# One batched graph kernel: the transposed operator scaled by a row instead of transposed on TensorE

## The chip, the core and the metric

The kernel runs on one core of one Trainium2 chip. The metric is the device time of one execution in microseconds (us). The time before is 292.79 us, the median of three runs (292.77 to 293.01). The engines in the profile are PE (TensorE matmuls), PEld (TensorE's weight loads), DVE (VectorE), ACT (ScalarE), POOL (GpSimd) and SP (SyncE, which here only issues DMAs).

## The reference

There are 64 graphs of 128 nodes, with 256 features each. For each graph, H is the 128 x 128 matrix of "adj is not zero", w is the first row of adj, and

```python
Dn = where(H @ w > 0, 1 / (H @ w), 0)            # one number per node
Be = 1 / H.sum(axis=0)                           # one number per hyperedge
def conv(x, W, b): return Dn * (H @ (Be * (H.T @ (x @ W.T)))) + b
h = layer_norm(relu(conv(x, W1, b1)))            # 256 -> 512 features
y = conv(h, W2, b2)                              # 512 -> 256 features
out = layernorm(x + (y + x))
```

With S = H B H^T (B the diagonal of Be) and D the diagonal of Dn, both convolutions apply A = D S to the nodes. S is symmetric, so A^T = S D: row i of A is row i of S times D_i, and column i of A^T is column i of S times D_i.

## The kernel before

The 64 graphs are handled in 16 groups of 4 (`PER = 4`, `G = 16`). Each engine has its own instruction stream, written out by hand, with semaphores between the streams; nothing is scheduled by a compiler, so the order in the code is the order on the engine. The main loop runs over i = 0 to 15; here one pass of it is called **stage i**. Stage i finishes group i and prepares the groups after it.

For a group j the steps are: `make_h` (DVE: H in bf16), `turn_h` (from group 3 on a DMA transpose issued by SP), `read_ht` (ACT: H^T, with the column sums), `make_b` (DVE: 1/column sums, `binv`), `make_htb` (ACT: B H^T), `copy_w` (POOL: w as a last column), `make_s` (PE: S and the node degrees, in PSUM tile `bank_s`), `make_d` (DVE: `dinv`, the D of the group, one value per node on its partition), `make_a` (ACT: A = D S, four instructions, one per graph), `turn_a` (PE: four transposes of A, against `ident`), `read_at` (ACT: A^T from PSUM into `at_sb`). A^T is what TensorE needs as weights: `make_u` multiplies it with x, and `make_y` with the hidden layer. The scaling D must be on the row index of A, which in S's own layout is a number per partition (cheap: `scale=dinv`), and in A^T's layout a number per column.

After that come `make_u` (PE), `split_u` (ACT and DVE: u as a high and a low part), `make_v` (PE, four blocks k = 0 to 3, three products each), `relu` and `square` (ACT), `split_r` (POOL makes `r_hi`, DVE `r_lo`), `add_pair` and `add_pairs` (DVE: sums of squares, `q_sb`), `turn_q` (PE transposes `q_sb`), `sum_q` (ACT), `make_g` (PE, one per graph), `make_var1` (DVE, four tiny instructions per half of a group), `inverse_std1` (POOL: a power of -0.5), `read_g` (DVE), `make_y` (PE, in two halves), `make_z` (DVE: y + 2 * `xb_sb`), `take_stats2` and `make_var2` (DVE), `inverse_std2` (POOL: a power and `shift2`), `normalise` (ACT), `store` (SP). `add_b2` (POOL) makes `xb_sb` = x + b2/2.

TensorE's order in a middle stage i is: make_g of graphs 0 and 1, make_v(i+1, 0), make_g of graph 2, make_v(i+1, 1), make_g of graph 3, make_v(i+1, 2), make_v(i+1, 3), **turn_a(i+2)**, make_y(i, 0), make_y(i, 1), make_s(i+3), make_u(i+2), turn_q(i+1). Two of its waits: the two halves of make_y use the PSUM banks that the last two blocks of make_v used, so half 1 waits until `relu` has read block 3:

```python
pe.wait_ge(g_ready, i * 2 + (half + 1))
pe.wait_ge(relu_ready, (i + 1) * KH + 3 + half)
```

And turn_q(i+1) waits for `q_ready`, DVE's last addition of squares.

SP works through one list of DMAs in order; in stage i these are load_adj(i+6), turn_h(i+4), load_x(i+3) and store(i-1), each with its own wait, and what is behind a waiting one waits too.

## Time and profile before

| | |
|---|---|
| median of three runs | 292.79 us |
| the profiled execution | 292.85 us |
| its span, first to last instruction | 291.0 us |
| PE busy | 279.9 us (96%) |
| DVE busy | 225.9 us (78%) |
| ACT busy | 210.4 us (72%) |
| POOL busy | 137.8 us (47%) |
| granted TensorE clock, mean | 0.993 of full |
| DMA, mean | 83 GB/s |

A timeline row has its start, its duration, the engine, the line, the operation and the tiles, how many instructions it merges, and in brackets, where there was one, the idle time before it with what ended it. Start times are from the span's start. Durations of neighbours overlap a little, since an instruction starts before the one ahead of it has drained; so the time that an instruction takes from its engine is read as the distance from its start to the next start, and its duration says when its result is there.

### The profile page before, as it was taken

The numbers are of one execution on the slowest core, as the hardware profiler recorded it, in microseconds if no ns is written. First come the engines' busy times: TensorE is split into PE (matmuls) and PEld (weight loads), VectorE is DVE, ScalarE is ACT, GpSimd is POOL, SyncE is SP. The second block draws the span as 40 slices with busy tenths as digits, with TensorE's granted clock in tenths as the row PEclk, the third lists the DMA queues.
The fourth block names the chain that finished last, engine by engine and source line by source line (L and its number), as shares of the span: only waits on it lengthen the run. The fifth ranks groups of instructions, "written<-read, shape, count | busy, mean of one in ns | idle before, by whom it ended". The sixth has DMA issues, their size and how long they took to land.

```text
span 291.0 us, 5897 instructions
## 1 busy us (share of the span) xinstructions
PE 279.9 (96%) x1866; PEld 254.4 (87%) x1866; DVE 225.9 (78%) x647; ACT 210.4 (72%) x621; POOL 137.8 (47%) x178
## 2 busy tenths in 40 slices
PE   7799999999999999999999999999999999999991
PEld 6689979898998989898998989899898989889880
DVE  1776689696978878697878969797897969587784
ACT  3397968868696887868687886868688785764514
POOL 2223763745454563645365374535446364426332
PEclk9999999999999999999999999999999999999997
DMA  6922040523406060321506051221406101020204
GB/s 222 303 78 50 8 126 0 123 79 77 124 18 182 0 199 2 119 83 29 170 3 199 2 156 43 77 88 23 145 0 185 53 31 44 0 74 0 72 3 144
DMA packets 33511, 24.28 MB, mean 83 GB/s; under 512 B 7932, under 2 KB 33224, under 8 KB 33480
## 3 DMA queue, kind: packets, MB, share of 16 engines
q1 hardware_dynamic: 33376, 23.86, 27.7%
q8 instruction: 15, 0.25, 0.4%
q14 instruction: 16, 0.13, 0.2%
q10 hardware_dynamic: 104, 0.04, 0.1%
HBM read 13.80 MB, written 8.39 MB: 76 GB/s over the span
## 4 chain that ended last, share of the span: by engine, by line
PE 85%; DVE 7%; issue 2%; POOL 2%; ACT 2%; DVEq 0%; POOLq 0%; ACTq 0%
PE bank_v L274 28%; PE bank_v L259 10%; PE bank_g L291 9%; PE bank_g L284 9%; PE bank_g L286 9%; PE bank_v L308 8%; PE bank_s L238 5%; PE bank_s L245 2%; PE bank_g L301 2%; DVE g_sb L636 1%; POOL rstd L840 1%; PE bank_s L341 1%; DVE binv L601 1%; ACT ht_sb L429 1%; DVE r_lo L645 1%
## 5 line engine op out<-in xcount | busy, mean ns | idle before, releaser
L851 POOL TENSOR_TENSOR xb_sb<-x_sb,b_half 128x1024 f32<-128x1024 f32 x16 | 38.4, 2400 | 58.9 <-DVE r_lo L645 53.8
L284 PE MATMUL bank_g<-w_hi,r_hi 128*128 128x258 f32 x256 | 65.6, 289 | 0.0
L286 PE MATMUL bank_g<-w_lo,r_hi 128*128 128x256 f32 x256 | 63.8, 282 | 0.0
L859 POOL TENSOR_SCALAR r_hi<-r_sb 128x512 fp32r<-128x512 f32 x64 | 48.0, 751 | 27.9 <-ACT r_sb L466 27.5
L636 DVE SCALAR_TENSOR_TENSOR g_sb<-bank_g,rstd,c 128x256 f32<-128x256 f32 x64 | 28.1, 480 | 30.7 <-POOL rstd L840 30.7
L274 PE MATMUL bank_v<-u_hi,w_hi 128*128 128x512 f32 x128 | 50.8, 397 | 0.4 <-DVE u_lo L609 0.4
L274 PE MATMUL bank_v<-u_hi,w_lo 128*128 128x512 f32 x128 | 50.8, 397 | 0.0
L274 PE MATMUL bank_v<-u_lo,w_hi 128*128 128x512 f32 x128 | 50.6, 395 | 0.0
L284 PEld LDWEIGHTS bank_g<-w_hi,r_hi 128*128 128x128 f32 x256 | 48.4, 189 | 1.4
L286 PEld LDWEIGHTS bank_g<-w_lo,r_hi 128*128 128x128 f32 x256 | 48.1, 188 | 1.2
L466 ACT ACTIVATE r_sb<-bank_v,vec 128x512 f32<-128x512 f32 x64 | 43.8, 684 | 7.2 <-PE bank_v L274 6.8
L460 ACT ACTIVATE u_hi<-bank_v 128x512 fp32r<-128x512 f32 x32 | 19.2, 599 | 38.5 <-PE bank_v L259 38.5
L645 DVE TENSOR_TENSOR r_lo<-r_sb,r_hi 128x512 fp32r<-128x512 f32 x64 | 43.3, 697 | 1.0 <-POOL r_hi L859 1.0
L478 ACT ACTIVATE z_sb<-z_sb,shift,rstd 128x256 f32<-128x256 f32 x60 | 32.5, 590 | 15.3 <-POOL shift L874 15.3
L291 PE MATMUL bank_g<-w_hi,r_lo 128*128 128x258 f32 x256 | 41.3, 283 | 0.0
L473 ACT ACTIVATE sq_sb<-r_sb 128x512 f32<-128x512 f32 x64 | 40.2, 634 | 1.5
L291 PEld LDWEIGHTS bank_g<-w_hi,r_lo 128*128 128x128 f32 x256 | 35.2, 189 | 0.0
L866 POOL TENSOR_TENSOR rstd<-var,half_power 128x4 f32<-128x4 f32 (+1 forms) x17 | 17.1, 1005 | 32.1 <-DVE var L693 32.1
L259 PE MATMUL bank_v<-at_sb,x_sb 128*128 128x128 f32 x256 | 31.5, 276 | 0.8 <-ACT at_sb L454 0.7
L259 PEld LDWEIGHTS bank_v<-at_sb,x_sb 128*128 128x128 f32 x256 | 29.8, 192 | 1.6 <-ACT at_sb L454 0.9
L840 POOL TENSOR_TENSOR rstd<-stat,half_power 128x2 f32<-128x2 f32 x32 | 22.6, 706 | 17.9 <-DVE stat L626 17.9
L308 PE MATMUL bank_v<-g_sb,at_sb 128*128 128x256 f32 x120 | 28.9, 381 | 0.6 <-DVE g_sb L636 0.6
(98 smaller groups left out, 489.2 us busy)
## 6 DMA issues: line engine op xcount, KB each, us to landing
x_sb<-in_x_dram SPq DMA_DIRECT2D x16, 512.0 KB, 3.9
out_dram<-z_sb SPq DMA_DIRECT2D x15, 512.0 KB, 3.2
adj_sb<-in_adj_dram SPq DMA_DIRECT2D x16, 256.0 KB, 3.9
w_raw<-in_L_gnn_W_dram SPq DMA_DIRECT2D x2, 512.0 KB, 5.7
out_dram<-z_sb SPq DMA_DIRECT2D x2, 256.0 KB, 2.6
turned_h<-h_sb SPq DMA_TRANSPOSE x13, 2.4
b_half<-in_L_gnn_b_dram SPq DMA_DIRECT2D x1, 128.0 KB, 8.8
edge_rows<-in_adj_dram ACTq DMA_DIRECT2D x1, 32.0 KB, 3.4
```

The lines of the kernel that those rows point to most:

```text
L259: mm = pe.matmul(bank_v[:, c, graph(n)], x_sb[:, j % 3, n, graph(c)], at_sb[:, j % 3, n], start=True, stop=True)
L274: mm = pe.matmul(bank_v[:, k % 2], w[:, c, graph(k)], u[:, c], start=(m == 0), stop=(m == len(terms) - 1))
L284: pe.matmul(bank_g[:, n, 0:W2COLS], r_hi[:, i % 2, k, graph(n)], w2_hi[:, k], start=(k == 0), stop=False)
L286: pe.matmul(bank_g[:, n, 0:DOUT], r_hi[:, i % 2, k, graph(n)], w2_lo[:, k], start=False, stop=False, skip_group_check=True)
L291: mm = pe.matmul(bank_g[:, n, 0:W2COLS], r_lo[:, i % 2, k, graph(n)], w2_hi[:, k], start=False, stop=(k == KH - 1))
L308: mm = pe.matmul(bank_v[:, half, (n % 2) * DOUT:(n % 2 + 1) * DOUT], at_sb[:, i % 3, n], g_sb[:, n], start=True, stop=True)
L466: nc.scalar.activation(r_sb[:, k], bank_v[:, k % 2], ACT.Relu, bias=vec[:, k:k + 1]).then_inc(relu_ready, 1)
L473: nc.scalar.activation(sq_sb[:, k], r_sb[:, k], ACT.Square).then_inc(sq_ready, 1)
L478: ins = nc.scalar.activation(z_sb[:, i % 2, n], z_sb[:, i % 2, n], ACT.Identity, bias=shift2[:, n:n + 1], scale=rstd2[:, 0, n:n + 1])
L645: nc.vector.tensor_tensor(r_lo[:, i % 2, k], r_sb[:, k], r_hi[:, i % 2, k].bitcast(F32), ALU.subtract).then_inc(r_lo_ready, 1)
L851: nc.gpsimd.tensor_tensor(xb_sb[:, i % 2], x_sb[:, i % 3], b2_half[:, :].unsqueeze(1).to_broadcast([P, PER, DOUT]), ALU.add).then_inc(xb_r ...
L859: nc.gpsimd.tensor_scalar(r_hi[:, i % 2, k], r_sb[:, k], 1.0, 1.0, ALU.mult, ALU.mult).then_inc(r_hi_ready, 1)
```

## The change

For groups 3 to 15 (`ON_PE = 3` says how many keep the old way) A is no longer made or transposed. A^T is made directly as S D: DVE multiplies S, read from PSUM, with a tile `d_row` that holds D along the free axis, the same on every partition, and writes `at_sb`. To get D from "one value per partition" to "a row on all partitions", SP stores `dinv` (128 x 4 values) to a DRAM tensor and loads it back broadcast to 128 partitions. Around this:

- `make_a` (ACT), `turn_a` (PE) and `read_at` (ACT) go for j >= 3. The new `make_at` stands on DVE between `make_var1(i, 1)` and `read_g(i, 1)`.
- `make_d(i+2)` moves ahead of `split_u(i+1)` on DVE. `make_var1(i, 0)` moves ahead of `make_var2(i-1)`, `read_g(i, 0)` ahead of `make_h(i+4)`, and on POOL `inverse_std1(i, 0)` ahead of `inverse_std2(i-1)`.
- `add_b2` is made in two halves and one stage later: in stage i now for group i, the first half after DVE's last `split_r`, the second after `make_b(i+3)`. The last group's is made in one piece after stage 14.
- ACT's `normalise(i-1, ...)` moves back: the first half from behind block 0 to behind block 1, the second from behind block 1 to behind block 3.
- `load_x` waits for the two halves of `xb_ready`.

The diff, cut:

```diff
-        dinv = sb("dinv", [P, PER])
+        dinv = sb("dinv", [P, 2, PER])
+        d_row = sb("d_row", [P, 2, P * PER])
...
+            def store_d(j):
+                sp.wait_ge(d_ready, j + 1)
+                sp.dma_start(d_rows[j], dinv[:, j % 2]).then_inc(d_stored, 16)
+
+            def load_d(j):
+                sp.wait_ge(d_stored, 16 * (j - ON_PE + 1))
+                if j >= ON_PE + 2:
+                    sp.wait_ge(at_ready, j - 1)
+                sp.dma_start(d_row[:, j % 2], d_rows[j].rearrange("c n -> (c n)").unsqueeze(0).to_broadcast(
+                    [P, P * PER])).then_inc(d_row_in[j % 2], 16)
...
                     load_adj(i + 6)
+                if i and i + 2 < G:
+                    store_d(i + 2)
+                    load_d(i + 2)
                 if i + 4 < G:
                     turn_h(i + 4)
...
                 make_v(i + 1, 3)
-                if i + 2 < G:
-                    turn_a(i + 2)
+                if i == 0:
+                    turn_a(2)
                 make_y(i, 0)
...
-                    if i + 2 < G:
-                        make_a(i + 2)
                     if i + 3 < G:
                         make_htb(i + 3)
                     relu(i + 1, 0)
                     square(i + 1, 0)
-                    normalise(i - 1, 0)
                 relu(i + 1, 1)
                 square(i + 1, 1)
                 if i:
-                    normalise(i - 1, 1)
+                    normalise(i - 1, 0)
                 relu(i + 1, 2)
                 square(i + 1, 2)
                 relu(i + 1, 3)
-                if i + 2 < G:
-                    read_at(i + 2)
+                if i == 0:
+                    read_at(2)
                 square(i + 1, 3)
+                if i:
+                    normalise(i - 1, 1)
...
+            def make_at(j):
+
+                dve.wait_ge(d_row_in[j % 2], 16 * (j // 2 if j % 2 else (j - 2) // 2))
+                dve.wait_ge(s_made, j + 1)
+                dve.wait_ge(y_made, (j - 2) * 2)
+                nc.vector.tensor_tensor(at_sb[:, j % 3].rearrange("p (b n) c -> p b n c", b=2),
+                                        s_parts[:, :, :, 0:P],
+                                        d_row[:, j % 2].rearrange("p (c b n) -> p b n c", b=2, n=2),
+                                        ALU.mult).then_inc(at_ready, 1)
...
+            def add_b2(i, half=None):
+
+                part, n = graphs(half), len(each(half))
+                if half != 1:
+                    pool.wait_ge(x_in[i % 3], landed(i, 3))
+                    if i >= 2:
+                        pool.wait_ge(z_ready, (i - 1) * 2)
+                    if i in (0, LAST):
+                        pool.wait_ge(q_ready, i + 1)
+                    else:
+                        pool.wait_ge(r_lo_ready, (i + 1) * KH)
+                elif i + 3 < G:
+                    pool.wait_ge(b_ready, i + 4)
...
-            add_b2(0)
...
-                add_b2(i + 1)
+                for half in range(2):
+                    add_b2(i, half)
+                inverse_std1(i, 0)
                 if i:
                     inverse_std2(i - 1)
-                inverse_std1(i, 0)
...
+            add_b2(LAST)
             for half in range(2):
                 inverse_std1(LAST, half)
```

How the instructions stand on the engines, from one middle stage to the next. First DVE at the start of a stage, before: the last two `split_r` of the old stage (`r_lo`), then `split_u`, `make_d` (three rows, `degree` and `dinv`), `make_b` (two rows, `binv`), `take_stats2` and `make_var2` (`mv_sb`, `mean`, `var`), and `make_var1` from `stat` on.

```order
L645 TENSOR_TENSOR r_lo<-r_sb,r_hi 128x512 x2
L609 TENSOR_TENSOR u_lo<-bank_v,u_hi 128x512 x2
L590 TENSOR_SCALAR degree<-bank_s 128x4
L592 RECIPROCAL degree<-degree 128x4
L596 SCALAR_TENSOR_TENSOR dinv<-bank_s,degree 128x4
L601 TENSOR_SCALAR binv<-members 128x4
L604 RECIPROCAL binv<-binv 128x4
L679 BN_STATS bn_sb<-z_sb 128x6 x4
L689 BN_AGGR mv_sb<-bn_sb 128x2 x4
L692 TENSOR_SCALAR mean<-mv_sb 128x4
L693 TENSOR_SCALAR var<-mv_sb 128x4
L615 TENSOR_SCALAR stat<-bank_g 128x2
```

The same place after:

```order
L661 TENSOR_TENSOR r_lo<-r_sb,r_hi 128x512 x2
L604 TENSOR_SCALAR degree<-bank_s 128x4
L606 RECIPROCAL degree<-degree 128x4
L612 SCALAR_TENSOR_TENSOR dinv<-bank_s,degree 128x4
L625 TENSOR_TENSOR u_lo<-bank_v,u_hi 128x512 x2
L617 TENSOR_SCALAR binv<-members 128x4
L620 RECIPROCAL binv<-binv 128x4
L695 BN_STATS bn_sb<-z_sb 128x6 x4
L631 TENSOR_SCALAR stat<-bank_g 128x2
```

`make_d` now stands ahead of `split_u`, and `make_var1` directly behind the four BN_STATS.

Second, DVE in the later part of a stage, before: the end of `make_var1(i, 1)` (three of its rows), `read_g(i, 1)` (`g_sb`), then `split_r`, the first `add_pair` and the two `make_z`.

```order
L618 TENSOR_TENSOR stat<-stat 128x2
L622 SCALAR_TENSOR_TENSOR stat<-sum_sq,stat 128x2
L626 TENSOR_SCALAR stat<-stat 128x2
L636 SCALAR_TENSOR_TENSOR g_sb<-bank_g,rstd,c 128x256 x2
L645 TENSOR_TENSOR r_lo<-r_sb,r_hi 128x512
L650 TENSOR_TENSOR pair_sb<-sq_sb 128x512
L671 SCALAR_TENSOR_TENSOR z_sb<-xb_sb,bank_v 128x512 x2
```

After:

```order
L634 TENSOR_TENSOR stat<-stat 128x2
L638 SCALAR_TENSOR_TENSOR stat<-sum_sq,stat 128x2
L642 TENSOR_SCALAR stat<-stat 128x2
L756 TENSOR_TENSOR at_sb<-bank_s,d_row 128x512
L652 SCALAR_TENSOR_TENSOR g_sb<-bank_g,rstd,c 128x256 x2
L661 TENSOR_TENSOR r_lo<-r_sb,r_hi 128x512
L666 TENSOR_TENSOR pair_sb<-sq_sb 128x512
L687 SCALAR_TENSOR_TENSOR z_sb<-xb_sb,bank_v 128x512 x2
```

One instruction is added, between the last row of `make_var1` and `read_g`.

Third, POOL over the turn of a stage, before: `copy_w` (`htb_sb`), `add_b2` (`xb_sb`), `inverse_std2` (`rstd2`, `shift2`), `inverse_std1` (`rstd1`), `split_r` (`r_hi`).

```order
L834 COPY htb_sb<-edge_cols 128x4
L851 TENSOR_TENSOR xb_sb<-x_sb,b2_half 128x1024
L866 TENSOR_TENSOR rstd2<-var2,half_power 128x4
L874 TENSOR_TENSOR shift2<-mean2,rstd2 128x4
L840 TENSOR_TENSOR rstd1<-stat1,half_power 128x2
L859 TENSOR_SCALAR r_hi<-r_sb 128x512 x2
```

After:

```order
L864 COPY htb_sb<-edge_cols 128x4
L886 TENSOR_TENSOR xb_sb<-x_sb,b2_half 128x512 x2
L870 TENSOR_TENSOR rstd1<-stat1,half_power 128x2
L901 TENSOR_TENSOR rstd2<-var2,half_power 128x4
L909 TENSOR_TENSOR shift2<-mean2,rstd2 128x4
L894 TENSOR_SCALAR r_hi<-r_sb 128x512 x2
```

The piece of 128x1024 is two of 128x512, and the power of the first half of `rstd1` goes ahead of `rstd2` and `shift2`.

## Rows read from the trace of the kernel before

**Rows 1.** The page, section 1: busy us, share of the span, instructions.
```profile
PE 279.9 (96%) x1866; PEld 254.4 (87%) x1866; DVE 225.9 (78%) x647; ACT 210.4 (72%) x621; POOL 137.8 (47%) x178
```
**Rows 2.** Stretches (us): busy PE, PEld, DVE, ACT, POOL; clock, DMA share, GB/s.
```profile
128.33:144.95 16.62, 16.62 (x116) 15.29 (x114) 13.77 (x40) 13.02 (x40) 8.43 (x10) 1.00 0.31 88
60.00:240.00 180.00, 180.00 (x1215) 165.55 (x1215) 145.91 (x425) 141.88 (x427) 91.21 (x108) 1.00 0.28 82
```
**Rows 3.** Timeline of PE, end of stage 6: turn_a, make_y, then turn_q.
```profile
139.75 0.60 PE L245 MATMUL bank_s<-ident,a_sb 128*128 128x128 f32 x4
140.19 1.89 PE L308 MATMUL bank_v<-g_sb,at_sb 128*128 128x256 f32 x8
...
144.59 0.60 PE L301 MATMUL bank_g<-ident,q_sb 128*128 128x128 f32 x4
```
**Rows 4.** Timeline of PEld: the weight load of turn_q in stage 6.
```profile
144.50 0.45 PEld L301 LDWEIGHTS bank_g<-ident,q_sb 128*128 128x128 f32 x4
```
**Rows 5.** Timeline of DVE, stage 6 and the start of stage 7.
```profile
138.37 0.17 DVE L626 TENSOR_SCALAR stat<-stat 128x2 f32<-128x2 f32 x1
139.44 0.88 DVE L636 SCALAR_TENSOR_TENSOR g_sb<-bank_g,rstd,c 128x256 f32<-128x256 f32 x2 [0.89 <-POOL rstd L840]
...
140.82 1.10 DVE L650 TENSOR_TENSOR pair_sb<-sq_sb 128x512 f32<-128x512 f32 x1
...
143.76 0.69 DVE L657 TENSOR_TENSOR q_sb<-pair_sb 128x512 f32<-128x512 f32 x1
...
147.61 0.65 DVE L601 TENSOR_SCALAR binv<-members 128x4 f32<-128x4 f32 x1 [0.28 <-ACT ht_sb L429]
```
**Rows 6.** Timeline of POOL, same stretch: r_hi of block 3, then xb.
```profile
140.72 0.67 POOL L859 TENSOR_SCALAR r_hi<-r_sb 128x512 fp32r<-128x512 f32 x1 [0.73 <-ACT r_sb L466]
...
145.83 2.40 POOL L851 TENSOR_TENSOR xb_sb<-x_sb,b_half 128x1024 f32<-128x1024 f32 x1 [3.86 <-DVE r_lo L645]
```
**Rows 7.** Stage 14, which has no turn_a: timelines of PE, PEld, ACT, DVE, POOL.
```profile
272.48 2.13 PE L308 MATMUL bank_v<-g_sb,at_sb 128*128 128x256 f32 x8
...
273.48 0.73 PEld L308 LDWEIGHTS bank_v<-g_sb,at_sb 128*128 128x128 f32 x4 [0.38 <-issue]
...
272.68 0.69 ACT L466 ACTIVATE r_sb<-bank_v,vec 128x512 f32<-128x512 f32 x1
...
273.14 0.68 DVE L650 TENSOR_TENSOR pair_sb<-sq_sb 128x512 f32<-128x512 f32 x1
...
273.45 0.85 POOL L859 TENSOR_SCALAR r_hi<-r_sb 128x512 fp32r<-128x512 f32 x1 [0.76 <-ACT r_sb L466]
```
**Rows 8.** Groups by form: DVE's product-like instruction of the nearest shape.
```profile
L609 DVE TENSOR_TENSOR u_lo<-bank_v,u_hi 128x512 fp32r<-128x512 f32 x32 | 20.6, 684 | 0.4 <-ACT u_hi L460 0.4
```
**Rows 9.** DMAs: issue to landing, median us.
```profile
adj_sb<-in_adj_dram SPq DMA_DIRECT2D x16, 256.0 KB, 3.9
...
out_dram<-z_sb SPq DMA_DIRECT2D x2, 256.0 KB, 2.6
...
b_half<-in_L_gnn_b_dram SPq DMA_DIRECT2D x1, 128.0 KB, 8.8
```
**Rows 10.** Stage 0: timelines of DVE (make_b) and PE (make_y, then make_s).
```profile
31.95 2.29 DVE L601 TENSOR_SCALAR binv<-members 128x4 f32<-128x4 f32 x1 [1.55 <-ACT ht_sb L429]
...
39.36 1.03 PE L308 MATMUL bank_v<-g_sb,at_sb 128*128 128x256 f32 x4
40.95 1.13 PE L308 MATMUL bank_v<-g_sb,at_sb 128*128 128x256 f32 x4 [0.56 <-DVE g_sb L636]
41.92 1.06 PE L238 MATMUL bank_s<-htb_sb,ht_sb 128*128 128x129 f32 x8
```
**Rows 11.** The end, stage 15: timelines of DVE (q_sb, stat, g_sb) and PE.
```profile
276.08 0.69 DVE L657 TENSOR_TENSOR q_sb<-pair_sb 128x512 f32<-128x512 f32 x1
...
278.72 0.16 DVE L618 TENSOR_TENSOR stat<-stat 128x2 f32<-128x2 f32 x1
...
283.68 1.13 PE L414 MATMUL bank_s<-g_sb,at_sb 128*128 128x256 f32 x4 [0.24 <-DVE g_sb L636]
```

More of the change, by code:

```diff
@@ L111, in hypergraph_block @@
         SUM = DOUT
-        turned_a = [bank_h] + [bank_q] * (G - 1)
+        ON_PE = 3
+        turned_a = [bank_h] + [bank_q] * (ON_PE - 1)
+        d_rows = nc.dram_tensor("d_rows", [G, P, PER], F32, kind="Internal").ap()
         turned_q = bank_g[:, PER - 1]
-        ON_PE = 3
         weights_in = [sem(f"weights_in{n}") for n in range(4)]
@@ L129, in hypergraph_block @@
         h_dma_turned = sem("h_dma_turned")
+        d_stored, d_row_in = sem("d_stored"), [sem("d_row_even"), sem("d_row_odd")]
         b_step, b_ready, htb_ready, wcol_ready = sem("b_step"), sem("b_ready"), sem("htb_ready"), sem("wcol_ready")
@@ L170, in load_x @@
                     sp.wait_ge(u_made, (j - 2) * KD)
-                    sp.wait_ge(xb_ready, j - 2)
+                    sp.wait_ge(xb_ready, (j - 2) * 2)
                 sp.dma_start(x_sb[:, j % 3], x_dram[:, j * PER:(j + 1) * PER]).then_inc(x_in[j % 3], 16)
@@ L234, in make_s @@
                 if j:
-                    pe.wait_ge(a_ready, j)
+                    pe.wait_ge(a_ready, min(j, ON_PE))
                     pe.wait_ge(at_ready, j)
@@ L401, in _ @@
             pe.wait_ge(consts_ready, 5)
-            pe.wait_ge(xb_ready, G)
+            pe.wait_ge(xb_ready, G * 2)
             for n in range(PER):
@@ L446, in make_a @@
                     ins = nc.scalar.activation(a_sb[:, n], s_parts[:, n // 2, n % 2, 0:P], ACT.Copy,
-                                               scale=dinv[:, n:n + 1])
+                                               scale=dinv[:, j % 2, n:n + 1])
                 ins.then_inc(a_ready, 1)
@@ L451, in read_at @@
                 act.wait_ge(a_turned, j + 1)
-                if j >= 3:
-                    act.wait_ge(y_made, (j - 2) * 2)
                 nc.scalar.activation(at_sb[:, j % 3].rearrange("p n c -> p (n c)"), turned_a[j],
@@ L593, in make_d @@
                 dve.wait_ge(degree_step, j * 2 + 2)
-                if j:
-                    dve.wait_ge(a_ready, j)
-                nc.vector.scalar_tensor_tensor(out=dinv[:, :], in0=degrees, scalar=0.0, in1=degree[:, 1],
+                if ON_PE > j >= 2:
+                    dve.wait_ge(a_ready, j - 1)
+                elif j >= ON_PE + 2:
+                    dve.wait_ge(d_stored, 16 * (j - 2 - ON_PE + 1))
+                nc.vector.scalar_tensor_tensor(out=dinv[:, j % 2], in0=degrees, scalar=0.0, in1=degree[:, 1],
                                                op0=ALU.is_gt, op1=ALU.mult).then_inc(d_ready, 1)
@@ L667, in make_z @@
                         dve.wait_ge(stored[i % 2], landed(i - 2, 2))
-                    dve.wait_ge(xb_ready, i + 1)
+                    dve.wait_ge(xb_ready, (i + 1) * 2)
                 dve.wait_ge(y_made, i * 2 + (half + 1))
@@ L729, in make_a @@
                 for n in range(PER):
-                    ins = nc.vector.tensor_scalar(a_sb[:, n], s_parts[:, n // 2, n % 2, 0:P], dinv[:, n:n + 1], None,
+                    ins = nc.vector.tensor_scalar(a_sb[:, n], s_parts[:, n // 2, n % 2, 0:P], dinv[:, j % 2, n:n + 1],
+                                                  None,
                                                   ALU.mult)
                 ins.then_inc(a_ready, 1)
+            def make_at(j):
[6 more added lines that the diff above has]
+                                        ALU.mult).then_inc(at_ready, 1)
             make_h(0)
@@ L765, in _ @@
                     add_squares(0)
+                if i and i + 2 < G:
+                    make_d(i + 2)
                 split_u(i + 1)
@@ L768, in _ @@
                     make_b(3)
-                if i + 2 < G:
-                    make_d(i + 2)
+                    make_d(2)
                 if i:
@@ L775, in _ @@
                     take_stats2(i - 1, 1)
+                make_var1(i, 0)
                 if i:
                     make_var2(i - 1)
-                make_var1(i, 0)
+                read_g(i, 0)
                 if i + 4 < G:
                     make_h(i + 4)
-                read_g(i, 0)
                 split_r(i + 1, 0)
                 make_var1(i, 1)
+                if i and i + 2 < G:
+                    make_at(i + 2)
                 read_g(i, 1)
@@ L841, in inverse_std1 @@
                                         ALU.pow).then_inc(rstd1_ready, 1)
-            def add_b2(i):
-                pool.wait_ge(x_in[i % 3], landed(i, 3))
-                if i >= 2:
-                    pool.wait_ge(z_ready, (i - 1) * 2)
-                if i:
-                    pool.wait_ge(r_lo_ready, i * KH)
-                else:
-                    pool.wait_ge(q_ready, 1)
-                nc.gpsimd.tensor_tensor(xb_sb[:, i % 2], x_sb[:, i % 3],
-                                        b2_half[:, :].unsqueeze(1).to_broadcast([P, PER, DOUT]),
-                                        ALU.add).then_inc(xb_ready, 1)
+            def add_b2(i, half=None):
[10 more added lines that the diff above has]
+                    pool.wait_ge(b_ready, i + 4)
+                nc.gpsimd.tensor_tensor(xb_sb[:, i % 2, part], x_sb[:, i % 3, part],
+                                        b2_half[:, :].unsqueeze(1).to_broadcast([P, n, DOUT]),
+                                        ALU.add).then_inc(xb_ready, 2 if half is None else 1)
             def split_r(i, k):
```

## The prediction

> **What bounds the kernel now.** I read the page's busy times first: PE is busy 279.9 of 291.0 us, the others 47 to 78% [rows 1]. The busy time by stretch then says where: from 60 to 240 us PE is busy all 180.00 us at full clock, and stage 6 takes 16.62 us, all of it PE [rows 2]. So in the middle a stage costs what TensorE's instructions cost, and only something that shortens its list, or makes it wait, moves the time.
>
> The timelines come next, because a busy engine can still be about to wait. At the end of stage 6 turn_a starts at 139.75, make_y at 140.19, turn_q at 144.59 [rows 3]. The weight load of turn_q starts at 144.50 [rows 4], and what it waits for, q_sb on DVE, ends at 143.76 + 0.69 = 144.45 [rows 5]. PE does not wait, but it has only 0.05 us in hand: VectorE's chain from the second power to q_sb is as long as TensorE's from the same point. A shorter TensorE list alone would gain nothing, so the question is whether both chains get shorter.
>
> **Part 1, turn_a off TensorE.** It takes 140.19 - 139.75 = 0.44 us a stage [rows 3], in stages 1 to 13 (groups 3 to 15).
>
> **Part 2, the wait that appears behind it.** Half 1 of make_y may start only when relu has read block 3, and turn_a was part of the time that this took. Stage 14 of the kernel before has no turn_a and shows the bare sequence [rows 7]: make_y at 272.48, relu of block 3 from 272.68 to 273.37, the weight load of half 1 only at 273.48 after 0.38 idle, and the eight records last 2.13 us where stage 6 has 1.89 [rows 3]. So half 1 starts 0.24 us late. relu starts 0.20 us after make_v in any case, bound by TensorE, so this wait comes in all 13 stages: 0.44 - 0.24 = 0.20 us is left, 2.6 us in all. Its bounds are 0 (relu later still) and 0.44 (no wait).
>
> **Part 3, VectorE must be 0.20 us earlier at q_sb.** Three things lengthen its chain now. (a) make_b at 147.61 takes 0.65 us, since xb on POOL runs from 145.83 to 148.23 [rows 5, 6] and it ends just behind that; in two halves, the first is over by about 147.0 and the second waits for make_b. That frees about 0.45 us. (b) DVE waits for each of two powers, 0.89 us for the second [rows 5]; make_var1 ahead of make_var2 gives it something to do during the first. (c) The first pair_sb takes 1.10 us instead of 0.68 [rows 5, 7]: it starts at 140.82, after r_hi of block 3 at 140.72 [rows 6], and ends behind it. Relative to the end of make_v, r_hi starts at +0.97 in stage 6 and in stage 14 (140.72 - 139.75; 273.45 - 272.48), because relu sets it. pair_sb starts at +1.07 in stage 6 but at +0.66 in stage 14, where DVE had no make_b; there pair_sb takes 0.68 and r_hi the longer 0.85 [rows 7]. Whoever starts first delays the other.
>
> With (a) and (b) DVE is at the second make_var1 when TensorE allows it, as in stage 14, so I put pair_sb at +0.66, 140.41. Then, with 0.6 to 0.7 us for each instruction on 128 x 512 [rows 5, 8]: first make_z 141.0; the second needs half 1 of make_y, which now starts at 139.75 + 0.86 + 0.24 = 140.85 and has its result 1.03 later [rows 10], 141.9; pair_sb 142.5, q_sb 143.2 to 143.9. The weight load of turn_q now wants 144.50 - 0.44 + 0.24 = 144.30. That leaves 0.3 to 0.4 us, so TensorE stays the bound.
>
> The Trainium skill, SBUF — State Buffer, section "Who interferes with whom", says that a VectorE instruction with two SBUF inputs contends with a GpSimd instruction that reads SBUF and that the first to start keeps the port for its whole length; the trace agrees, in pair_sb against r_hi (1.10 and 0.68). By the same rule the new make_at, with one input in PSUM, should hinder nobody; no row shows that instruction.
>
> **Part 4, make_at.** The trace does not show it. The nearest row is u_lo, 128 x 512 from one PSUM and one SBUF tile, 0.684 us [rows 8]; d_row is read with a stride of four elements, which no row shows, so the upper end is twice that, 1.3. Below 0.6 I see nothing, since no row of DVE on 128 x 512 in fp32 is quicker. It lies between 138.54 (138.37 + 0.17) and read_g at 139.44 [rows 5], a gap of 0.9 for 0.68, so it costs nothing; at 1.3 it would eat 0.4, about the 0.3 above, and cost up to 0.1 a stage. On ACT four make_a and one read_at go, some 2 us a stage; ACT waits for TensorE before each relu, so nothing is gained.
>
> **Part 5, the row of D.** SP issues two DMAs that depend on each other. make_d, now ahead of split_u, is done about 0.9 us into the stage. Neither DMA is in the trace. Nearest rows: 2.6 us for a store of 256 KB, 3.9 for the load of adj, also 256 KB [rows 9]. Two in a row are 5.2 to 7.8, so d_row lands 6.1 to 8.7 us into the stage. make_at wants it at 138.5 - 128.33 = 10.2 by the rows of before, at 9.5 with the earlier make_var1. So it is in time, by 0.8 to 3.4 us. b_half, a small broadcast load queued behind the first big ones, took 8.8 [rows 9]; that is the far end. Behind the waiting load_d on SP stand turn_h, whose own wait (make_h) ends only 7 us into the stage, load_x and store, which have a stage to spare. The later normalise moves store(i-1) and load_adj to about 14 us into the stage, so they are mostly over when store_d is issued.
>
> The Trainium skill, DMA: Bandwidth & Descriptors, gives about 2.0 us fixed per DMA ("Anatomy of one DMA") and a read-modify-write for pieces under 512 bytes ("Specifications"). Two would be an estimated 4.6 us with 256 KB at its rate, in time as well, and the store's pieces of 16 bytes speak against the change; no row here shows what they cost.
>
> **Part 6, the ends.** Stage 0 keeps turn_a but loses a blocked make_b: 2.29 us behind two whole xb [rows 10] becomes about 0.2. There TensorE waited for read_g in make_y: from 39.36 to make_s at 41.92 are 2.56 us instead of 1.73 in stage 6, 0.83 too many. I take 0.8 back, with the small waits behind it (0.2 to 0.3) standing for what stays; bounds 0.4 and 1.1. At the end xb of group 15 moves from stage 14 behind q_sb: it starts about 276.8 (276.08 + 0.69) and runs 2.4 us to 279.2, over DVE's stat at 278.72 with its two SBUF inputs, which then ends 0.4 later [rows 11]. The last make_y waits for read_g already (0.24), so I pass on 0.35; bounds 0 and 0.5.
>
> **The sum.** Profiled execution 292.85 (span 291.0 plus 1.85 around it) - 13 x 0.20 - 0.80 + 0.35 = 289.80. The median is 0.06 below that execution, so 289.7.
>
> **Rivals.** *The chain on VectorE stays the bound.* If DVE reaches pair_sb after r_hi (+0.97), it is blocked again, q_sb ends at 144.45 as now, and turn_q cannot come earlier: a stage stays at 16.62, and only the ends count, 292.8 - 0.8 + 0.35 = 292.3. For it: 0.3 us is all that separates the two orders. Against: stage 14 shows the other order. *No new wait, the whole 0.44.* 292.8 - 5.7 - 0.8 + 0.35 = 286.6. Against: stage 14 again. *The row comes late, slower than before.* DVE is in order, so a late d_row holds read_g, pair_sb, make_z and q_sb. It begins to cost when the row lands more than 10 us into the stage and outweighs the gain from 10.9 on. At 11.5, make_at ends 12.2, read_g 13.0, r_lo, pair_sb, two make_z, pair_sb and q_sb bring q_sb's end to about 16.7 into the stage, against 16.12 now (144.45 - 128.33): 13 x 0.55 = 7.2 more, 299.5. For it: two DMAs of kinds that the trace does not have, and one row of 8.8. Against: both nearest rows leave room.
>
> **How the numbers follow.** Forecast 0.62, at 289.7, with its own range 288.9 to 290.6; VectorE's chain 0.16; the whole gain 0.08; the late row 0.14. The range takes in the forecast, the first rival and the upper part of the second, 288.2 to 292.7. A measurement of this kernel can tell about 0.2%, 0.6 us, from no change: faster is the forecast, the second rival and a fifth of the first, 0.73; the same 0.13; slower 0.14.
>
> **What would show it.** Right: stages of about 16.4 us; a wait of PE in make_y on relu (ACT, r_sb) in 13 more stages; no wait on q_sb in the middle; the first pair_sb at 0.68 with r_hi at 0.85; make_at at about 0.7 with no wait on a DMA; make_b near 0.17. Wrong: stages of 16.6 with turn_q waiting on q_sb (first rival); stages of 16.2 (second); DVE waiting on DMA d_row and stages above 16.8 (third). Most at risk are the landing of two small DMAs and the 0.3 us at pair_sb.

## The result, and the profile after

The changed kernel takes 289.75 us (median of four runs, 289.71 to 290.7) where the kernel before takes 292.78 (four runs beside it, 292.67 to 293.01). The ratio is 0.9896 with an interval of 0.9879 to 0.9913: 1% faster. The forecast was 289.7.

The times of most versions here, of before too, fall in two groups about 0.95 us apart. The profiled execution of after is in the longer one (290.7, span 288.9): its first make_g starts at 24.98, in the kernel before at 24.04. The difference arises ahead of the loop. Eight profiled executions of this study are of the longer group and start the loop at 24.97 to 25.51, the others at 24.03 or 24.04. In all eight the first make_s takes 1.9 to 2.1 us, in the others 1.16, though the profile gives the same granted clock of 1.00 for both; this is before and then after:

```profile
7.70 1.16 PE L238 MATMUL bank_s<-htb_sb,ht_sb 128*128 128x129 f32 x8 [0.31 <-DVE htb_sb L723]
```

```profile
7.80 1.99 PE L255 MATMUL bank_s<-htb_sb,ht_sb 128*128 128x129 f32 x8
```

Why is open. Below, stages are compared by their own length, which this doesn't touch.

The page of after, busy us by engine, answers to [rows 1]: 52 fewer instructions on PE, and 15 us less on ACT.

```profile
PE 277.7 (96%) x1814; PEld 249.0 (86%) x1814; DVE 227.9 (79%) x660; ACT 195.6 (68%) x556; POOL 138.6 (48%) x193
```

The middle is still all TensorE. This is one stage of after (stage 7, from 143.98; the window takes in 0.04 us of the next) and the stretch from 60 to 240 us, columns as in [rows 2]:

```profile
143.98:160.43 16.45, 16.44 (x112) 14.84 (x110) 13.81 (x41) 11.96 (x35) 8.39 (x11) 1.00 0.42 106
60.00:240.00 180.00, 179.93 (x1186) 162.28 (x1185) 150.71 (x439) 131.18 (x374) 92.25 (x120) 1.00 0.37 101
```

The timeline of PE at the end of stage 6 answers to [rows 3]. There is no turn_a, make_y takes 2.13 instead of 1.89 (in stage 7 too, from 155.39), and from turn_q to turn_q are 160.03 - 143.62 = 16.41 us, where before they were 16.62:

```profile
138.97 2.13 PE L325 MATMUL bank_v<-g_sb,at_sb 128*128 128x256 f32 x8
...
143.62 0.60 PE L318 MATMUL bank_g<-ident,q_sb 128*128 128x128 f32 x4
```

The weight loads of the same stretch (against [rows 4] and the PEld line of [rows 7]): half 1 of make_y waits 0.38 us, until 0.11 after relu of block 3 has ended on ACT (at 139.86), and the load of turn_q waits for nothing. The same 0.38 stands in each of the stages 1 to 14.

```profile
139.97 0.73 PEld L325 LDWEIGHTS bank_v<-g_sb,at_sb 128*128 128x128 f32 x4 [0.38 <-issue]
...
143.51 0.47 PEld L318 LDWEIGHTS bank_g<-ident,q_sb 128*128 128x128 f32 x4
```

DVE and POOL there answer to [rows 5, 6]. The first pair_sb is at 0.68, r_hi of block 3 at 0.85, and the new make_at is the line with `at_sb`:

```profile
136.38 0.16 DVE L631 TENSOR_SCALAR stat<-bank_g 128x2 f32<-128x2 f32 x1 [0.27 <-PE bank_g L308]
...
137.15 1.08 DVE L756 TENSOR_TENSOR at_sb<-bank_s,d_row 128x512 f32<-128x512 f32 x1
138.16 0.87 DVE L652 SCALAR_TENSOR_TENSOR g_sb<-bank_g,rstd,c 128x256 f32<-128x256 f32 x2
...
139.64 0.68 DVE L666 TENSOR_TENSOR pair_sb<-sq_sb 128x512 f32<-128x512 f32 x1
...
142.47 0.69 DVE L673 TENSOR_TENSOR q_sb<-pair_sb 128x512 f32<-128x512 f32 x1
```

```profile
137.29 0.71 POOL L870 TENSOR_TENSOR rstd<-stat,half_power 128x2 f32<-128x2 f32 x1 [0.71 <-DVE stat L642]
...
139.94 0.85 POOL L894 TENSOR_SCALAR r_hi<-r_sb 128x512 fp32r<-128x512 f32 x1 [0.76 <-ACT r_sb L481]
```

And the two new DMAs (KB, median us from issue to landing), with the issue of stage 6's on SP:

```profile
d_row<-d_rows SPq DMA_DIRECT2D x13, 256.0 KB, 3.4
d_rows<-dinv SPq DMA_DIRECT2D x13, 2.0 KB, 2.1
```

```profile
128.46 0.33 SPq L188 DMA_DIRECT2D d_rows<-dinv  x1
131.52 0.33 SPq L194 DMA_DIRECT2D d_row<-d_rows  x1
```

Where the 2.10 us between the two profiled spans (291.0 and 288.9) went, by the first make_g of each stage: the start +0.94 (the group of the execution, see above), stage 0 -0.68, stages 1 to 12 together -2.60, stage 13 -0.21, stage 14 nothing, stage 15 and the rest +0.45. Without the start, -3.04; the medians say -3.03.

Of the 2.60, each stage gives 0.20 or 0.21, together 2.46. The other 0.14 is one stage of the kernel before: in its profiled execution stage 7 took 16.76 us, not 16.62. There pair_sb started 1.25 us after the end of make_v (157.62 - 156.37), q_sb ended at 161.25, and turn_q had to wait for it. This is DVE and PEld of before:

```profile
157.62 1.10 DVE L650 TENSOR_TENSOR pair_sb<-sq_sb 128x512 f32<-128x512 f32 x1
...
160.56 0.69 DVE L657 TENSOR_TENSOR q_sb<-pair_sb 128x512 f32<-128x512 f32 x1
```

```profile
161.30 0.42 PEld L301 LDWEIGHTS bank_g<-ident,q_sb 128*128 128x128 f32 x4
```

### The profile page after: what moved, and what is told of

Same layout as the page of the kernel before. It is cut to its first block, busy times and chain, and to the rows that moved or that the text cites. A ratio compares the mean times of both kernels' runs of the same rounds, so it can differ in the third digit from the quotient of the medians.

```text
span 288.9 us, 5778 instructions
## 1 busy us (share of the span) xinstructions
PE 277.7 (96%) x1814; PEld 249.0 (86%) x1814; DVE 227.9 (79%) x660; ACT 195.6 (68%) x556; POOL 138.6 (48%) x193
## 4 chain that ended last, share of the span: by engine, by line
PE 85%; DVE 7%; issue 2%; POOL 2%; DMA 2%; ACT 1%; DVEq 0%; SPq 0%; POOLq 0%
PE bank_v L291 29%; PE bank_g L308 10%; PE bank_g L301 10%; PE bank_g L303 10%; PE bank_v L325 9%; PE bank_v L276 9%; PE bank_s L255 5%; PE bank_g L318 2%; DMA w_raw<-in_L_gnn_W_dram 2%; POOL rstd L870 1%; DVE g_sb L652 1%; DVE r_lo L661 1%; DVE pair_sb L666 1%; PE bank_g L333 1%; PE bank_g L353 1%
## 5 line engine op out<-in xcount | busy, mean ns | idle before, releaser
L886 POOL TENSOR_TENSOR xb_sb<-x_sb,b_half 128x512 f32<-128x512 f32 (+1 forms) x31 | 41.2, 1331 | 75.6 <-DVE r_lo L661 51.6
L661 DVE TENSOR_TENSOR r_lo<-r_sb,r_hi 128x512 fp32r<-128x512 f32 x64 | 44.7, 719 | 11.1 <-POOL r_hi L894 11.1
L325 PE MATMUL bank_v<-g_sb,at_sb 128*128 128x256 f32 x120 | 31.9, 388 | 0.1
L325 PEld LDWEIGHTS bank_v<-g_sb,at_sb 128*128 128x128 f32 x120 | 21.4, 189 | 8.6 <-issue 5.3
```

What stands on the lines that cost most here:

```text
L325: mm = pe.matmul(bank_v[:, half, (n % 2) * DOUT:(n % 2 + 1) * DOUT], at_sb[:, i % 3, n], g_sb[:, n], start=True, stop=True)
L661: nc.vector.tensor_tensor(r_lo[:, i % 2, k], r_sb[:, k], r_hi[:, i % 2, k].bitcast(F32), ALU.subtract).then_inc(r_lo_ready, 1)
L886: nc.gpsimd.tensor_tensor(xb_sb[:, i % 2, part], x_sb[:, i % 3, part], b2_half[:, :].unsqueeze(1).to_broadcast([P, n, DOUT]), ALU.add).the ...
```

## The experiments

The theory: the gain is turn_a's 0.44 less a wait of 0.24 on relu, times 13, and it can show only because DVE's chain got shorter. The rivals: DVE's chain was never the bound, so the moves do nothing; or the moves alone bring the gain. All edits are against the changed kernel. Each run is set against the kernel before on its own chip (292.81 beside the first four, 293.15 beside the next four, 293.1 beside the last two). The medians of before differ by 0.3 between the chips, and a median of few runs can fall into either of the two groups of times, so the ratio is given beside each time, and differences of a few tenths are read from the length of the stages in the traces.

**xb whole and a stage earlier, as before.**

```diff
-                for half in range(2):
-                    add_b2(i, half)
+                add_b2(i + 1)
                 inverse_std1(i, 0)
...
```

The diff is cut; add_b2's waits and its calls ahead of the loop and after it are as before the change too.

> The changed kernel, but xb again in one piece of 128x1024 and a stage earlier, as before the change (add_b2(i+1) at the start of stage i, behind the last split_r). Theory of the prediction, part 3a: make_b is blocked for 0.4 us again, pair_sb comes after r_hi of block 3 (more than 0.97 us after make_v), q_sb ends too late for turn_q, middle stages 16.6 us, in all about 292.0 to 292.4 (12 x 0.20 more, stage 0 0.7 more, the end 0.45 less than 289.75). Rival: 0.3 us of room at pair_sb is enough for a late make_b, stages stay at 16.42 and only the ends change: 289.75 + 0.7 - 0.45 = 290.0.

Measured: 292.62 (291.28 to 294.17, ten runs), ratio 0.9996 (0.9973 to 1.002). By the median the gain is gone, and a little more than the 292.0 to 292.4 of the theory. The profiled execution is one of the quicker ones (291.85), and it has stages of two kinds. In stage 6 (16.56 us) r_hi starts 0.09 ahead of pair_sb, in stage 7 (16.45) pair_sb goes at full speed; POOL and DVE of that kernel, POOL first:

```profile
141.39 0.65 POOL L889 TENSOR_SCALAR r_hi<-r_sb 128x512 fp32r<-128x512 f32 x1 [0.78 <-ACT r_sb L481]
...
157.96 1.28 POOL L889 TENSOR_SCALAR r_hi<-r_sb 128x512 fp32r<-128x512 f32 x1 [0.78 <-ACT r_sb L481]
```

```profile
131.63 0.72 DVE L617 TENSOR_SCALAR binv<-members 128x4 f32<-128x4 f32 x1 [0.21 <-ACT ht_sb L446]
...
141.48 1.10 DVE L666 TENSOR_TENSOR pair_sb<-sq_sb 128x512 f32<-128x512 f32 x1
...
158.05 0.72 DVE L666 TENSOR_TENSOR pair_sb<-sq_sb 128x512 f32<-128x512 f32 x1
```

So make_b behind a whole xb (0.72) puts pair_sb and r_hi on the same instant, and whichever wins sets the stage. Against after, from first make_g to first make_g, stage 0 is 1.25 longer (21.76 against 20.51, where the theory had 0.7), stages 1 to 6 together 1.29 (five of 16.56 or 16.57 and one of 16.95), stages 7 to 12 have after's 16.42, and the end gives 0.44 back. From stage 8 on make_b takes 0.33 to 0.44 and pair_sb is 0.3 ahead of r_hi again. So half of the middle stages kept the whole gain with a whole xb; the halves make sure of it. Executions with more or fewer stages of the long kind would explain the spread of 3 us between the runs, but only one was profiled. In the second pair the listed start of r_hi is the earlier one too, and yet it is r_hi that was slowed: at 0.09 us apart the order in the trace no longer tells who had the memory first.

**All the moves, but A still made and transposed on TensorE.**

```diff
-                if i == 0:
-                    turn_a(2)
+                if i + 2 < G:
+                    turn_a(i + 2)
```

with make_a and read_at on ACT for all groups, and without store_d, load_d and make_at.

> All the moves of the change (xb in halves and later, make_d, powers, normalise), but A made on ScalarE and transposed on TensorE in every group as before; no row of D, no make_at. Theory: TensorE's list is as long as before (turn_a 0.44 us, and no wait in make_y behind it), so middle stages stay at 16.62 us; stage 0 gains 0.7, the end loses 0.45: 292.8 - 0.25 = 292.5. Rival: the moves themselves made most of the gain: below 291.

Measured: 292.49 (292.46 to 293.76, ten runs), ratio 0.9992 (0.9978 to 1.0007). The moves alone bring nothing in the middle; two turn_q in a row are 16.62 apart, as before. Its PE:

```profile
128.49 0.60 PE L315 MATMUL bank_g<-ident,q_sb 128*128 128x128 f32 x4
...
140.71 1.89 PE L322 MATMUL bank_v<-g_sb,at_sb 128*128 128x256 f32 x8
...
145.11 0.60 PE L315 MATMUL bank_g<-ident,q_sb 128*128 128x128 f32 x4
```

The first two runs together: the shorter chain on VectorE gives nothing alone (ratio 0.9992); the shorter list on TensorE with xb whole gives nothing by the median (0.9996), though half of the middle stages of its profile had the gain; both together give 0.9896. A kernel that only drops turn_a, with none of the moves, was not run.

**The two powers in the old order.**

```diff
-                make_var1(i, 0)
                 if i:
                     make_var2(i - 1)
-                read_g(i, 0)
+                make_var1(i, 0)
                 if i + 4 < G:
                     make_h(i + 4)
+                read_g(i, 0)
```

and on POOL inverse_std2 ahead of inverse_std1 again.

> The changed kernel, but make_var2 and inverse_std2 again ahead of make_var1(i, 0) and inverse_std1(i, 0), and make_h ahead of read_g(i, 0). Theory of the prediction, part 3b: VectorE reaches the second make_var1 some 0.5 us later, pair_sb falls behind r_hi, stages 16.6 us, 292.0 to 292.4. Rival: part 3a alone gives enough room, stages 16.42, 289.75 within 0.3 (the end does not change, stage 0 may change a little).

Measured: 289.72 (289.67 to 291.17), ratio 0.9909 (0.9886 to 0.9932), stages of 16.42. The theory's claim falls here: the new order of the powers isn't needed. Of Part 3's (a) and (b), the halves of xb are enough (the moves of make_d and normalise stayed in). The order of the powers does give room: in stages 5 and 12 of this kernel pair_sb starts only 0.02 ahead of r_hi, in after always 0.3.

**make_s between the halves of make_y.** The wait on relu is to be filled with other work; the second add_pair goes ahead of the second make_z, which now comes later.

```diff
                 make_y(i, 0)
-                make_y(i, 1)
                 if i + 3 < G:
                     make_s(i + 3)
+                make_y(i, 1)
```

> The changed kernel with make_s(i+3) between the two halves of make_y on TensorE, and on VectorE the second add_pair ahead of the second make_z. Theory, part 2: the 0.24 us at half 1 of make_y is nothing but its wait for relu of block 3 behind a make_v with no cover; 0.89 us of make_s cover it. Then the wait goes in all stages, and what is late next is make_z of half 1 (half 1 starts 0.65 us later): make_u's second chunk waits for it about 0.15 us, so stages 16.2 to 16.35 and 288.0 to 289.0 in all. Rival: the 0.24 us is a fixed cost of the step from make_v to make_y (fp32 behind fp32r) and stays: 289.75, or more if the later make_z holds turn_q.

Measured: 289.32 (288.82, 288.87, 289.78, 289.85, so a median between the two groups; the shorter one is 0.9 below after's own), ratio 0.9884 (0.9866 to 0.9901), stages of 16.33. The wait is gone, a new one of some 0.15 comes behind: make_u now takes 2.10 instead of 1.95, since it needs the bank that the late second make_z reads. PE of that kernel:

```profile
138.83 1.02 PE L325 MATMUL bank_v<-g_sb,at_sb 128*128 128x256 f32 x4
139.69 1.06 PE L255 MATMUL bank_s<-htb_sb,ht_sb 128*128 128x129 f32 x8
140.58 1.03 PE L325 MATMUL bank_v<-g_sb,at_sb 128*128 128x256 f32 x4
141.45 2.10 PE L276 MATMUL bank_v<-at_sb,x_sb 128*128 128x128 f32 x16
143.39 0.60 PE L318 MATMUL bank_g<-ident,q_sb 128*128 128x128 f32 x4
```

**Half of make_s between the halves, the other half behind.** 0.45 us of work for a wait of 0.24.

```diff
                 make_y(i, 0)
+                if i + 3 < G:
+                    make_s(i + 3, 0)
                 make_y(i, 1)
                 if i + 3 < G:
-                    make_s(i + 3)
+                    make_s(i + 3, 1)
...
```

The diff is cut; make_s gets a half, and on VectorE the second add_pair goes ahead of the second make_z as in the run before.

> The changed kernel with TensorE's order make_y half 0, two graphs of make_s, make_y half 1, the other two graphs of make_s, and on VectorE the second add_pair ahead of the second make_z. With all of make_s between the halves the wait for relu went, but make_u waited 0.16 us for make_z (stage 16.33). Theory: half of make_s, 0.45 us, still covers the 0.24, and make_z is 0.45 us earlier, so no engine holds TensorE in a middle stage: 16.62 - 0.44 = 16.18 us, 12 x 0.24 under the changed kernel: 286.8 to 287.1. Rival: turn_q or make_u waits again (q_sb behind the later make_z): stages 16.3, 288.5 to 289.3.

Measured: 286.95 (286.84 to 288.03), ratio 0.9792 (0.9769 to 0.9815). PE of that kernel has no wait left in a stage, and two turn_q in a row are 16.17 apart:

```profile
138.15 1.02 PE L327 MATMUL bank_v<-g_sb,at_sb 128*128 128x256 f32 x4
139.01 0.61 PE L256 MATMUL bank_s<-htb_sb,ht_sb 128*128 128x129 f32 x4
139.46 1.03 PE L327 MATMUL bank_v<-g_sb,at_sb 128*128 128x256 f32 x4
...
142.55 0.60 PE L320 MATMUL bank_g<-ident,q_sb 128*128 128x128 f32 x4
...
158.72 0.60 PE L320 MATMUL bank_g<-ident,q_sb 128*128 128x128 f32 x4
```

16.62 - 16.17 = 0.45 is turn_a's whole 0.44. So the wait of Part 2 is what the change pays, and it can be had back.

**The row of D loaded twice, one after the other.** The row comes one DMA later.

```diff
+                sp.dma_start(d_row[:, j % 2], row).then_inc(d_first, 16)
+                sp.wait_ge(d_first, 16 * (j - ON_PE + 1))
                 sp.dma_start(d_row[:, j % 2], row).then_inc(d_row_in[j % 2], 16)
...
```

The diff is cut; `row` is the broadcast view of D in DRAM.

> The changed kernel, with d_row loaded twice, the second load behind the landing of the first, and make_at waiting for the second. In the trace of the changed kernel the row lands 3.4 us after its issue at 131.52, at 134.9, and make_at starts at 137.15: 2.2 us in hand. The second load takes 3.4 to 3.9 more, so it lands 1.2 to 1.7 us after make_at wants it. Theory (the third rival of the prediction, its turning point): VectorE waits for the DMA in each stage, pair_sb falls behind r_hi and q_sb is late: stages 16.9 to 17.5 us, 296 to 303 in all. Rival: the second load is short or VectorE makes the delay good, since it still waits for make_y and for relu later: stages 16.4 to 16.6, under 292.5.

Measured: 293.59 (291.6 to 295.82, ten runs), ratio 1.001 (0.9983 to 1.0036). DVE of stage 6, and the line of that kernel's waits (us in total, times, longest):

```profile
138.78 1.12 DVE L759 TENSOR_TENSOR at_sb<-bank_s,d_row 128x512 f32<-128x512 f32 x1 [1.14 <-DMA d_row<-d_rows]
...
143.95 0.69 DVE L676 TENSOR_TENSOR q_sb<-pair_sb 128x512 f32<-128x512 f32 x1
```

```profile
DVE at_sb L759 <- DMA d_row<-d_rows: 8.7, 13, 1.1
```

The result lies below what the theory expected and above the rival. A late row does hold read_g and all behind it, as the third rival had it, and takes the whole gain. But 8.7 us of waits in the profiled execution (293.96, its loop starting at 24.04) cost some 4.2 against the 289.73 of after's shorter group: turn_q to turn_q is 144.72 - 127.60 = 17.12 in one stage and 16.46 in the next, so in part of the stages the delay is absorbed by what DVE has in hand. That other executions absorb it in other stages would explain the spread of 4 us; it was not shown, since one was profiled.

**The row read without the stride of four.** This leaves the product with the wrong columns of D; it is there for the time of make_at alone.

```diff
-                                        d_row[:, j % 2].rearrange("p (c b n) -> p b n c", b=2, n=2),
+                                        d_row[:, j % 2].rearrange("p (b n c) -> p b n c", b=2, n=2),
```

> The changed kernel, with make_at reading d_row densely (graph, then node) instead of with a stride of four elements; the values of D then stand at the wrong columns, the work is the same. Theory: the 1.07 us of make_at, where u_lo of the same size takes 0.68, are the stride; dense it takes 0.68 to 0.75 and the time of the kernel stays, 289.7 within 0.2, because make_at ends just when the second power is there (read_g starts 0.06 us after the power's result plus its usual 0.10). Rival: the 1.07 comes from the PSUM side (four pieces of 128) and stays.

Measured: 289.72 (289.7 to 289.76), ratio 0.9878 (0.9863 to 0.9894). Groups by form (count, shortest/median/longest ns, first and last start), of after and then of this kernel:

```profile
L756 DVE TENSOR_TENSOR at_sb<-bank_s,d_row x13: 1061/1075/1086, 55.1 to 252.0; 128x512 f32<-128x512 f32 x13
```

```profile
L756 DVE TENSOR_TENSOR at_sb<-bank_s,d_row x13: 691/692/692, 54.1 to 251.1; 128x512 f32<-128x512 f32 x13
```

The stride costs 0.38 us an instruction and nothing in time: read_g follows make_at's start by 1.01 in after (138.16 - 137.15) and by 0.95 here (137.13 - 136.18), because here it waits for the power.

```profile
136.18 0.69 DVE L756 TENSOR_TENSOR at_sb<-bank_s,d_row 128x512 f32<-128x512 f32 x1
137.13 0.88 DVE L652 SCALAR_TENSOR_TENSOR g_sb<-bank_g,rstd,c 128x256 f32<-128x256 f32 x2 [0.26 <-POOL rstd L870]
```

**xb of group 15 in stage 14.** An attempt to take back the +0.45 at the end.

```diff
                 for half in range(2):
                     add_b2(i, half)
+                if i == LAST - 1:
+                    add_b2(LAST)
...
```

The diff is cut; the call after the loop goes.

> The changed kernel, with xb of the last group made in stage 14, behind the two halves of group 14, instead of after q_sb of stage 14. Theory (the end of the sum): in the changed kernel xb of the last group holds stat on VectorE for 0.64 us instead of 0.16 and the last make_y waits 0.70 instead of 0.24; this comes back, 289.3, minus 0.45. Rival: the same 2.4 us of xb now hold VectorE's small instructions in stage 14 and are paid there: 289.7 or more.

Measured: 290.47 (289.99 to 291.42), ratio 0.9904 (0.9873 to 0.9935): no gain, the theory's claim falls and its rival holds. The hold moved to a worse place. POOL and DVE of stage 14 in that kernel:

```profile
259.42 4.90 POOL L886 TENSOR_TENSOR xb_sb<-x_sb,b_half 128x512 f32<-128x512 f32 x3 [3.74 <-DVE r_lo L661]
```

```profile
262.12 2.21 DVE L638 SCALAR_TENSOR_TENSOR stat<-sum_sq,stat 128x2 f32<-128x2 f32 x1
...
271.32 1.10 DVE L666 TENSOR_TENSOR pair_sb<-sq_sb 128x512 f32<-128x512 f32 x1
```

An instruction that takes 0.16 alone took 2.21: it ended at 264.33, where the last of the three pieces of xb, the whole one of group 15, ended too (259.42 + 4.90). DVE then reached pair_sb behind r_hi. The last turn_q came 5.42 after make_y (269.92 to 275.34), in after 4.84 (269.93 to 274.77); from there to the end it was 0.37 shorter, so the end did get better, by less than stage 14 lost.

**xb of group 15 in two halves, the second behind the first power; alone, and with make_s split.**

```diff
-            add_b2(LAST)
             for half in range(2):
+                add_b2(LAST, half)
                 inverse_std1(LAST, half)
...
```

The diff is cut; the last matmuls wait for each half of xb apart.

> The changed kernel, with xb of group 15 in two halves on GpSimd: the first where the whole one is now (behind q_sb of group 15), the second behind the first power of group 15; the last step's matmuls wait for each half apart. Theory (the end is 0.45 us longer than before because the whole xb, 2.40 us, holds VectorE's 128x2 stat with two SBUF inputs for 0.64 instead of 0.16): the first half (about 1.27) is over before that stat starts, so it takes 0.16, the first power, both read_g and the end come 0.3 to 0.48 us earlier, median 289.3 to 289.45. In the profile: stat at 0.16 about 1.05 us behind turn_q, the second half of xb at 1.27 behind the power. Rival (the hold only moves): the second half meets the stat of the second variance, which then takes 0.3 to 0.6 instead of 0.16, and read_g of the second half, on which the last matmuls wait, is no earlier: 289.7.

> The version with make_s split around the halves of make_y (run before at 286.95), and xb of group 15 in two halves as in the run beside this one. The two edits touch different stretches, stages 0 to 12 the one and the end the other, so by the theory they add: 286.95 less 0.3 to 0.48, median 286.5 to 286.65. Rival (the hold only moves to the second variance): 286.9 to 287.0. If both edits worked on the same wait, this would show less than their sum.

Measured: alone 290.21 (five runs: 289.27, 289.30, 290.21, 290.26, 290.39), ratio 0.9884 (0.9864 to 0.9903). As a median that misses the theory's 289.3 to 289.45, but it fell into the longer of the two groups of times here; group against group it is 289.3 against after's 289.73, and 290.3 against 290.7, 0.4 less. With make_s split: 286.48 (286.38 to 287.41), ratio 0.9767 (0.9751 to 0.9782), against 286.95 without, 0.47 less. The traces show the cause: stat is at 0.16 again, and the last matmuls wait 0.23 for g_sb where in after they wait 0.70. POOL, DVE and PE of the run alone:

```profile
274.42 1.29 POOL L887 TENSOR_TENSOR xb_sb<-x_sb,b_half 128x512 f32<-128x512 f32 x1 [2.64 <-DVE q_sb L674]
```

```profile
276.20 0.16 DVE L635 TENSOR_TENSOR stat<-stat 128x2 f32<-128x2 f32 x1
```

```profile
281.18 1.13 PE L432 MATMUL bank_s<-g_sb,at_sb 128*128 128x256 f32 x4 [0.23 <-DVE g_sb L653]
```

and the same three of after, beside [rows 11]:

```profile
274.39 2.40 POOL L886 TENSOR_TENSOR xb_sb<-x_sb,b_half 128x1024 f32<-128x1024 f32 x1 [2.64 <-DVE q_sb L673]
```

```profile
276.17 0.64 DVE L634 TENSOR_TENSOR stat<-stat 128x2 f32<-128x2 f32 x1
```

```profile
281.60 1.13 PE L431 MATMUL bank_s<-g_sb,at_sb 128*128 128x256 f32 x4 [0.70 <-DVE g_sb L652]
```

The version with both edits is the best of this study, 2.3% faster than before, and 1.1% (by the times) to 1.3% (by the ratios) faster than the change itself.

## Why the prediction was right, point by point

- **Part 1 and 2, the middle.** Right, and to the hundredth: make_y's eight records last 2.13 in every such stage, half 1's weight load starts 1.00 after the end of make_v (139.97 - 138.97) as in stage 14 of before (273.48 - 272.48), the stage is 16.41 to 16.42, and each of the stages 1 to 12 gave 0.20 or 0.21. That the wait is really the price was shown by splitting make_s: the other 0.24 a stage came back. Stage 13 gave 0.21 too, but by another way than the working had. It has no make_s any more, and there turn_q does wait for q_sb, before (first row) and after (second): the stage goes by DVE's chain, not by TensorE's list. DVE waits there for make_y (0.26 before, 0.23 after), whose result is there 2.13 after the end of make_v instead of 2.33 (0.44 + 1.89), and so turn_q comes after 4.24 (258.11 - 253.87) instead of 4.44 (260.66 - 256.22). That this is the same 0.20 is no merit of the working.

```profile
260.66 0.42 PEld L301 LDWEIGHTS bank_g<-ident,q_sb 128*128 128x128 f32 x4 [0.16 <-DVE q_sb L657]
```

```profile
258.11 0.42 PEld L318 LDWEIGHTS bank_g<-ident,q_sb 128*128 128x128 f32 x4 [0.32 <-DVE q_sb L673]
```

- **The room before.** The 0.05 us "in hand" were read from stage 6 alone. In stage 13, where the profile says that the load of turn_q waits for q_sb, it starts 0.06 after q_sb's end as well (260.66 against 260.60), so 0.05 is more likely the hand-over than room. On the other side stages 2, 3, 4 and 12 of before had 0.35, since pair_sb took 0.69 there; all the other middle stages had 0.05 to 0.09, and stage 7 was late by 0.14. The conclusion stands for two stages out of three.
- **Part 3, the race.** pair_sb was put at +0.66 after make_v with 0.68, and is at 139.64 - 138.97 = 0.67 with 0.68; r_hi at +0.97 with 0.85. The room at turn_q was given as 0.3 to 0.4, and is 143.51 - (142.47 + 0.69) = 0.35. Of the three reasons, (a) is what made it sure in every stage and (c) is what it works through (the run with a whole xb); (b) is not (the run with the old order of the powers), although the text made it part of the condition. The first rival, 292.3, has its mechanism in the run with a whole xb: where r_hi holds pair_sb up, turn_q comes 0.05 behind q_sb and the stage is 16.56 or longer. The number of that run (292.62) is near the rival's by luck: no middle stage of it has the 16.62 that the rival counts, half of them have 16.42, its stage 0 is 0.57 longer than that of before (21.76 against 21.19) where the rival has it 0.8 shorter, and its end costs nothing.
- **Part 4, make_at.** The step that was mis-sized: 1.075 us, taken as 0.68, with 1.3 as the upper end. The stride is the cause. It cost 0.06 a stage on DVE (1.01 against 0.95) out of 0.35 in hand, and no time. It also hindered nobody, as was expected: POOL's power of `rstd` ran beside it (137.29) in 0.71, as in every stage of before.
- **Part 5, the row.** 2.1 and 3.4 us, where 2.6 and 3.9 were taken. In stage 6 it lands at 131.52 + 3.4 = 134.9, and is wanted at 137.15: 2.2 us in hand. That is 7.3 into the stage (134.9 - 127.56), inside the 6.1 to 8.7 of the working. The estimate by the Trainium skill, DMA: Bandwidth & Descriptors (4.6 for both), is 0.9 below the trace (2.1 + 3.4); the page fits its fixed 2.0 us to DMAs that GpSimd issues, and these are SP's. The pieces of 16 bytes showed no harm at 2 KB. The third rival's mechanism exists (the row loaded twice), and it was priced too low. In stage 6 of that run make_at started 10.8 into the stage (138.78 - 127.99, its first make_g), for which the working gives a stage of about 16.5, still shorter than before; measured were 17.12. From make_at's start to q_sb's end are 5.86 us (144.64 - 138.78), where the working has 5.2 (11.5 to 16.7), and the stride of make_at is 0.4 of the difference. The whole came to 293.59 and not more because other stages absorbed their part.
- **Part 6, the ends.** Stage 0 gave 0.68 (taken 0.80), the end cost 0.45 (taken 0.35), the hold of stat being 0.64 as foreseen; both inside their bounds. Two halves of xb take back 0.4 to 0.5 of it.

The terms were off by little: stages 1 to 13 gave 2.67 where 2.60 was taken, stage 0 gave 0.12 less and the end cost 0.10 more. By these alone the sum would have been 0.15 too low. It came out within 0.05 because the profiled execution of before, from which it starts, had 0.14 of delay in stage 7 that the working didn't know of. So the last tenth is luck.

## What to carry to other kernels

When two engines' chains are equally long, a change of one alone can show nothing: price both, and give the gain as what the shorter of the two new distances allows. Look for a stage of the same kernel that already lacks the step you remove (here stage 14 without turn_a); it shows the wait that will appear. And when a removed step leaves a short wait, look for half of an independent step to put there: all of it brought a new wait, half of it brought everything.

## What the runs showed of the hardware

- VectorE multiplying 128 x 512 in fp32 with an SBUF operand read at a step of 16 bytes takes 1.075 us, the same with a step of 4 bytes 0.692.
- A VectorE instruction with two SBUF inputs that comes while POOL works through xb waits however small it is: a 128x2 stat took 0.64 behind the whole xb at the end, and 2.21 behind the same piece in stage 14, instead of 0.16. The Trainium skill, SBUF — State Buffer, section "Who interferes with whom", says that the first to start keeps the port for its whole length, which these agree with. make_b, 128x4 with one SBUF input, was held as well: 0.65 to 0.72 behind a whole xb, 2.29 behind two, 0.17 in after.
- Where two such instructions start within 0.1 us of each other, either can be the one that is slowed: with xb whole it was pair_sb in stage 6 and r_hi in stage 7, r_hi starting 0.09 earlier in both. The times of that version spread over 3 us (291.28 to 294.17), where versions without such a tie mostly repeat within 0.2 inside their group; before had the tie too without that spread, since its stage was 16.62 both ways, but for stage 7.
- Storing 128 pieces of 16 bytes to DRAM lands in 2.1 us, and one row of 2 KB broadcast to 128 partitions in 3.4.
